# Fetching the embedded rows of five steps by indirect transfers instead of one-hot products

## The reference, cut to what matters

```
h = take(weight.T, x)                                   # (64, 128, 64)
# attention over the heads (h = 8), on the layer-normalised h, no softmax over keys:
q, k, v = (ln(h) @ Wq, ln(h) @ Wk, ln(h) @ Wv)
attn = sigmoid(einsum('bifh,bjfh->bijh', q, k) * 8)
h = h + relu(einsum('bijh,bjfh->bifh', attn, v) @ Wo)
# mixture of 6 experts, 2 per token, on the layer-normalised h:
gates = softmax(top2(softmax(relu(ln(h) @ Wr1 + b) @ Wr2 + b)))
h = h + sum over the 2 chosen experts of gate * expert(ln(h))   # 3 layers of 64 x 64
```

## Time and profile before

| | us |
|---|---|
| median of three runs | 260.37 (257.58 to 261.57) |
| the profiled execution: its own time | 258.21 |
| its span, first to last instruction | 256.4 |
| end of the first part (last `Htab` instruction ends) | 111.96 |
| DVE's `variance` of iterations 2, 3, 4, 5, 6 starts at | 148.03, 162.18, 176.79, 191.16, 205.01 |

### The profile page before, as it was taken

One profiled execution on the slowest core, in us unless ns is written; L12 is line 12 of the kernel. 1 busy time (PEld: TensorE's weight loads), 2 busy tenths in 40 slices (PEclk: granted clock), 3 DMA queues, 4 the chain that ended last, 5 costly groups with the idle time before them and its releaser, 6 DMA issues.

```text
span 256.4 us, 5843 instructions
## 1 busy us (share of the span) xinstructions
PE 206.5 (81%) x2356; PEld 87.8 (34%) x2356; DVE 161.7 (63%) x331; ACT 104.3 (41%) x188; POOL 80.9 (32%) x122
## 2 busy tenths in 40 slices
PE   0559775899899899954837688999899979999882
PEld 0336431234335343344616142524234323232220
DVE  4352852335977857963586488887979685754261
ACT  1148321233453452502431715556273644534430
POOL 4000664322642633044536071532505050101010
PEclk9999997599999799985577799999999999999998
DMA  7541799999898896200006775393938577594911
GB/s 152 129 144 24 182 228 243 252 251 247 222 256 199 233 254 173 82 0 3 0 1 149 163 181 123 88 215 98 206 95 183 123 158 148 119 186 114 202 36 41
DMA packets 25770, 37.85 MB, mean 148 GB/s; under 512 B 15376, under 2 KB 16592, under 8 KB 25744
## 3 DMA queue, kind: packets, MB, share of 16 engines
q1 hardware_dynamic: 18864, 19.92, 34.8%
q0 software_dynamic: 5216, 16.98, 25.9%
q10 hardware_dynamic: 1664, 0.58, 1.1%
HBM read 17.79 MB, written 2.83 MB: 80 GB/s over the span
## 4 chain that ended last, share of the span: by engine, by line
PE 46%; DVE 19%; DMA 14%; ACT 6%; POOL 5%; issue 5%; SPq 4%; DVEq 0%; ACTq 0%
PE PS L644 10%; PE PS L668 9%; PE PS L807 6%; DMA xb<-ids_scratch 6%; DMA G<-Gs 5%; PE PS L778 5%; PE PS L794 4%; POOL st L388 4%; ACT H L482 3%; DVE lead L1064 2%; DVE Htab L925 2%; SPq L335 2%; PE PS L680 2%; DVE OH L992 2%; DVE st L1026 2%
## 5 line engine op out<-in xcount | busy, mean ns | idle before, releaser
L228 POOL DMA_DIRECT2D G<-Gs x64 | 33.5, 529 | 59.3 <-ACT Gs L466 54.2
L644 PE MATMUL PS<-A,BD 32*32 32x256 f32 x1024 | 35.6, 415 | 9.5 <-ACT Gs L466 7.2
L1043 DVE SCALAR_TENSOR_TENSOR H2g<-PS,nb_s,WB 128x1024 f32<-128x1024 f32 x24 | 30.7, 1280 | 11.2 <-PE PS L794 11.2
L482 ACT ACTIVATE H<-PS,b_s 128x512 f32<-128x512 f32 x48 | 30.2, 681 | 16.6 <-PE PS L778 16.5
L969 DVE COPY Gs<-PS 128x512 f32<-128x512 f32 x32 | 20.9, 686 | 20.6 <-PE PS L644 13.1
L668 PE MATMUL PS<-G,cnt 128*64 128x512 f32 x128 | 32.2, 637 | 0.0
L794 PE MATMUL PS<-H,W2s 64*64 64x512 f32 x192 | 27.0, 634 | 5.7 <-ACT H L482 5.6
L466 ACT ACTIVATE Gs<-PS 128x512 f32<-128x512 f32 x32 | 17.6, 595 | 33.0 <-PE PS L644 30.2
L778 PE MATMUL PS<-X,W1s 64*128 64x512 f32 x96 | 27.7, 655 | 0.7 <-ACT H L482 0.7
L807 PE MATMUL PS<-H2g,W3s 128*64 128x512 f32 x96 | 25.5, 616 | 0.4 <-DVE H2g L1043 0.4
L644 PEld LDWEIGHTS PS<-A,BD 32*32 32x32 f32 x1024 | 16.3, 108 | 25.4 <-issue 11.2
(11 more groups left out here) (112 smaller groups left out, 306.4 us busy)
## 6 DMA issues: line engine op xcount, KB each, us to landing
G<-Gs POOLq DMA_DIRECT2D x64, 256.0 KB, 6.4
WB<-gate_scratch SPq DMA_DIRECT2D x16, 768.0 KB, 7.7
xb<-ids_scratch SPq DMA_DIRECT2D x8, 256.0 KB, 7.4
h_out<-Y SPq DMA_DIRECT2D x8, 256.0 KB, 7.0
GG<-gate_scratch SPq DMA_DIRECT2D x64, 12.0 KB
vo_scratch<-VOs SPq DMA_DIRECT2D x2, 256.0 KB, 2.1
VOr<-vo_scratch SPq DMA_DIRECT2D x4, 128.0 KB, 3.0
wk_s<-wk SPq DMA_DIRECT2D x2, 128.0 KB, 4.7
```

Of the source, the lines that this page charges most:

```text
L228: eng.dma_start(G2[half % G2_RING][first::8, :, :], Gs[n % GS_RING][:, m, :]).then_inc(sent[n % GS_RING][m], 16)
L482: ins = act.activation(H1[q][:, u * HT:(u + 1) * HT], PS[:, B_L1 + u, :], ACT.Relu, bias=b1_s[:, u, q:q + 1])
L644: ins = pe.matmul(PS[32 * x:32 * x + 32, B_G + i, w * NV:(w + 1) * NV], BD[n % BD_RING][rows, x].rearrange("p c f -> p (c f)")[:, w::2], A ...
L1043: dve.scalar_tensor_tensor(out=H2g[q][:], in0=two_banks(l2_bank(q)), scalar=nb2_s[:, q:q + 1], in1=WB[s % RING][:, q, :], op0=ALU.max, op1 ...
```

## The change

The one-hot product is kept for steps 0, 1 and 2 (`ON_PE = 3`). For steps 3 to 7:

- SP stores the part of `Htab` that belongs to sequences 24 to 63 in device memory (`h_scratch`, two transfers of 1.31 MB), as soon as the table is complete and ahead of all transfers of the loop.
- DVE computes row numbers once (`row_of` = id x 40 + sequence - 24).
- POOL fetches: `fetch(i + 3)` in iterations 0 to 4, each eight indirect transfers of 128 rows of 256 bytes, straight into `H2` in float32. `centre(i)` and POOL's `normalise(i - 1)` wait for all eight to have landed.
- Gone for these five steps: `gather`, `take_h`, `one_hot_ids`, `x_load` and `cut`; `Hmid`, `Hlo` and `rem` are made for 24 of the 64 sequences only.

Besides: `H2` has eight buffers in place of five; `WB` is loaded by six transfers of 256 KB in place of two of 768 KB, with a semaphore per pair of experts; PE issues `router(i)` ahead of `gather(i + 2)`; and in iterations 0 and 1 DVE issues `normalise(i + 1)` behind `two_best(i)`.

```diff
@@ -61,11 +62,13 @@
 RING = 4
-H_RING = 5
-
-
-C_ID, C_IOTA, C_MASK, C_SEL, C_BM, C_TIE, C_CA, C_CB, C_END = (
-    0, 128, 130, 138, 138 + 192, 334, 370, 370 + NC, 370 + 2 * NC)
+ON_PE = 3
+NBP = ON_PE * TB
+NBD = NB - NBP
+
+
+C_ID, C_IOTA, C_MASK, C_SEL, C_BM, C_TIE, C_CA, C_CB, C_ROW, C_END = (
+    0, 128, 130, 138, 138 + 192, 334, 370, 370 + NC, 370 + 2 * NC, 370 + 2 * NC + NBD)
 A_BITS, B_BITS = 0x33, 0xCC
@@ -78,6 +81,7 @@
     gate_dram = nc.dram_tensor("gate_scratch", (RING, E, TOK), F32, kind="Internal").ap()
+    h_dram = nc.dram_tensor("h_scratch", (NV * NBD, D), F32, kind="Internal").ap()
     ids_dram = nc.dram_tensor("ids_scratch", (1, NB * S), BF16, kind="Internal").ap()
@@ -95,7 +99,8 @@
         Htab = sb("Htab", [P, VK, NB, D])
-        Hmid, Hlo = sb("Hmid", [P, VK, NB, D], BF16), sb("Hlo", [P, VK, NB, D], BF16)
+        Hmid, Hlo = sb("Hmid", [P, VK, NBP, D], BF16), sb("Hlo", [P, VK, NBP, D], BF16)
+        row_of = sb("row_of", [P, NBD], U32)
         rb1_s = sb("rb1_s", [P, 1])
@@ -125,7 +130,7 @@
         O1 = [sb(f"O1{i}", [P, 512], F32, att) for i in range(2)]
-        rem = sb("rem", [P, VK, NB, FB], F32, att)
+        rem = sb("rem", [P, VK, NBP, FB], F32, att)
         G2 = [sb(f"G2{i}", [P, FB, NV], F32, att) for i in range(2)]
@@ -149,7 +154,7 @@
         rem_s = [sb(f"rem_s{i}", [P, VK, TB, FB]) for i in range(2)]
-        H2 = [sb(f"H2{i}", [P, TB, D]) for i in range(H_RING)]
+        H2 = [sb(f"H2{i}", [P, TB, D]) for i in range(STEPS)]
         xc = sb("xc", [P, TB, D])
@@ -307,15 +314,17 @@
             x_load(sp, 2)
+            sp.wait_ge(h_tab, NF * 4 * VK)
+            for k in range(VK):
+                sp.dma_start(h_dram[k * P * NBD:(k + 1) * P * NBD].rearrange("(p b) f -> p (b f)", b=NBD),
+                             Htab[:, k, NBP:, :].rearrange("p b f -> p (b f)")).then_inc(h_st, 16)
             for i in range(STEPS + LAG):
                 if i < STEPS:
-                    if i + 3 < STEPS:
-                        sp.wait_ge(oh_b, VK * (i + 2))
-                        x_load(sp, i + 3)
                     sp.wait_ge(gt_sb, i + 1)
                     if i >= RING:
-                        sp.wait_ge(wb_ld[i % RING], 32 * (i // RING))
+                        for q in range(PAIRS):
+                            sp.wait_ge(wb_ld[i % RING][q], 32 * (i // RING))
                         sp.wait_ge(gg_ld[i % RING], 128 * (i // RING))
@@ -323,10 +332,10 @@
                         sp.wait_ge(gp_ready, i - RING + 1)
-                    for e in range(2):
-                        src = gate_dram[i % RING].rearrange("(q e) k -> e q k", e=2)[e:e + 1]
-                        sp.dma_start(WB[i % RING][e * D:(e + 1) * D, :, :],
-                                     src.broadcast_to([D, PAIRS, TOK])).then_inc(wb_ld[i % RING], 16)
+                    for q in range(PAIRS):
+                        for e in range(2):
+                            src = gate_dram[i % RING][2 * q + e:2 * q + e + 1].broadcast_to([D, TOK])
+                            sp.dma_start(WB[i % RING][e * D:(e + 1) * D, q, :], src).then_inc(wb_ld[i % RING][q], 16)
                     if i == 0:
@@ -380,12 +389,28 @@
                 pool.wait_ge(ln_dve, 4 * i + 3)
-                pool.wait_ge(cut_pool, 3 * min(i + 1, STEPS - 1))
+                pool.wait_ge(cut_pool, 3 * min(i + 1, ON_PE - 1))
+                if ON_PE <= i + 1 < STEPS:
+                    pool.wait_ge(h_ld[i + 1], 16 * TB)
                 if i - 2 >= LAG:
                     pool.wait_ge(gp_ready, i - 1 - LAG)
                 pool.tensor_scalar(st[:, 2, :], st[:, 1, :], EPS, None, ALU.add).then_inc(ln_pool, 1)
                 pool.wait_ge(ln_pool, 2 * i + 1)
                 pool.tensor_tensor(st[:, 3, :], st[:, 2, :], mhalf[:], ALU.pow).then_inc(ln_pool, 1)
+
+            def fetch(i):
+
+                if i == ON_PE:
+                    pool.wait_ge(rows_ok, 1)
+                    pool.wait_ge(h_st, 16 * VK)
+                if i - 3 >= LAG:
+                    pool.wait_ge(gp_ready, i - 2 - LAG)
+                else:
+                    pool.wait_ge(ln_pool, 2 * (i - 1))
+                for t in range(TB):
+                    pool.indirect_dma_start(H2[i][:, t, :], None, h_dram,
+                                            bass.IndirectOffsetOnAxis(row_of[:, i * TB - NBP + t:i * TB - NBP + t + 1], 0))\
+                        .then_inc(h_ld[i], 16)
@@ -405,12 +430,8 @@
                         .then_inc(gp_ready, 1)
-                if i + 3 < STEPS:
-                    if s >= 0:
-                        pool.wait_ge(gp_ready, s + 1)
-                    else:
-                        pool.wait_ge(ln_pool, 2 * (i + 2))
-                    cut(i + 3)
+                if ON_PE <= i + 3 < STEPS:
+                    fetch(i + 3)
@@ -536,7 +555,7 @@
                     relu1(s + 1, 0)
-                if i + 2 < STEPS:
+                if i + 2 < ON_PE:
                     take_h(i + 2)
@@ -827,10 +846,10 @@
                     layer2(s, 0)
-                if i + 2 < STEPS:
-                    gather(i + 2)
                 if a:
                     router(i)
+                if i + 2 < ON_PE:
+                    gather(i + 2)
                 if b:
@@ -873,6 +892,8 @@
                    .then_inc(oh_ready, 1)
+            dve.scalar_tensor_tensor(out=row_of[:], in0=xt_i[:, NBP:], scalar=float(NBD), in1=cst[:, C_ROW:C_ROW + NBD],
+                                     op0=ALU.mult, op1=ALU.add).then_inc(rows_ok, 1)
             dve.wait_ge(ld_ids, 16)
@@ -950,7 +971,7 @@
                     dve.wait_ge(lo_ok, VK * (q - 1) + k + 1)
-                dve.tensor_tensor(rem[:, k], Htab[:, k, :, f], upper(Htab[:])[:, k, :, f], ALU.subtract)\
+                dve.tensor_tensor(rem[:, k], Htab[:, k, :NBP, f], upper(Htab[:])[:, k, :NBP, f], ALU.subtract)\
                    .then_inc(rem_ok, 1)
@@ -1015,11 +1036,14 @@
             def centre(i):
-                dve.wait_ge(h_sb, i + 1)
-                dve.tensor_reduce(st[:, 0, :], H2[i % H_RING][:], AX.X, ALU.add).then_inc(ln_dve, 1)
+                if i < ON_PE:
+                    dve.wait_ge(h_sb, i + 1)
+                else:
+                    dve.wait_ge(h_ld[i], 16 * TB)
+                dve.tensor_reduce(st[:, 0, :], H2[i][:], AX.X, ALU.add).then_inc(ln_dve, 1)
                 dve.wait_ge(ln_dve, 4 * i + 1)
                 dve.scalar_tensor_tensor(out=xc[:], in0=over(st[:, 0, :], D), scalar=-1.0 / D,
-                                         in1=H2[i % H_RING][:], op0=ALU.mult, op1=ALU.add).then_inc(ln_dve, 1)
+                                         in1=H2[i][:], op0=ALU.mult, op1=ALU.add).then_inc(ln_dve, 1)
@@ -1036,8 +1060,7 @@
                 dve.wait_ge(l2_ps, PAIRS * s + q + 1)
-                if q == 0:
-                    dve.wait_ge(wb_ld[s % RING], 32 * (s // RING + 1))
+                dve.wait_ge(wb_ld[s % RING][q], 32 * (s // RING + 1))
                 if s >= 1 and q == 0:
@@ -1118,8 +1141,8 @@
                     gate2(s, 0)
-                if ahead:
-                    normalise(i + 1)
+                    if ahead:
+                        normalise(i + 1)
                 if a:
@@ -1128,12 +1151,12 @@
                     gate2(s, 2)
+                else:
+                    normalise(i + 1)
                 if a:
                     gates(i)
                 if i + 2 < STEPS:
                     centre(i + 2)
-                if i + 3 < STEPS:
-                    one_hot_ids(i + 3)
                 if b:
```

More of the change, by code:

```diff
@@ L22 @@
 I32 = mybir.dt.int32
+U32 = mybir.dt.uint32
 ALU = mybir.AluOpType
@@ L194, in build @@
         oh_b, h_ps, h_sb = sem("oh_b"), sem("h_ps"), sem("h_sb")
+        rows_ok, h_st = sem("rows_ok"), sem("h_st")
+        h_ld = {i: sem(f"h_ld{i}") for i in range(ON_PE, STEPS)}
         rem_ok, mid_ok, lo_ok, cut_dve, cut_pool = (sem(n) for n in ("rem_ok", "mid_ok", "lo_ok", "cut_dve", "cut_pool"))
@@ L200, in build @@
         gate_st = [sem(f"gate_st{i}") for i in range(2)]
-        wb_ld = [sem(f"wb_ld{i}") for i in range(RING)]
+        wb_ld = [[sem(f"wb_ld{i}{q}") for q in range(PAIRS)] for i in range(RING)]
         gg_ld = [sem(f"gg_ld{i}") for i in range(RING)]
@@ L487, in take_h @@
                 act.wait_ge(h_ps, i + 1)
-                if i >= H_RING:
-                    act.wait_ge(y_sb, i - H_RING + 1)
-                act.activation(H2[i % H_RING][:].rearrange("p t f -> p (t f)"), PS[:, B_H, :], ACT.Copy)\
+                act.activation(H2[i][:].rearrange("p t f -> p (t f)"), PS[:, B_H, :], ACT.Copy)\
                    .then_inc(h_sb, 1)
@@ L1105, in result @@
                                   PS[:, B_Y, :].rearrange("p (j u o) -> p u j o", u=2, o=D),
-                                  H2[s % H_RING][:].rearrange("p (u j) o -> p u j o", u=2), ALU.add).then_inc(y_sb, 1)
+                                  H2[s][:].rearrange("p (u j) o -> p u j o", u=2), ALU.add).then_inc(y_sb, 1)
             cut()
```

(1 more changed line is left out.)

## The result

The changed kernel took 277.95 us at the median (276.58 to 281.99), the kernel before 260.85 (257.58 to 261.57): a ratio of **1.068, 95% interval 1.054 to 1.083**. It is slower, and outside the predicted range.

What follows compares the result with a forecast made beforehand. The loop was taken as bound by a 13.85 us round trip over four engines, not PE's load. The span 256.4 - 0.4 + 1.0 for the clock = 257.0 us gave 258.8 us, range 250 to 271.

Steps and rivals of the forecast that it cites:

- P(6): P(k) is the start of POOL's `normalise` of step k; for step 6, 191.55 us was forecast against 191.93 before.
- the formula's terms: Start of POOL's `normalise` of step 6 as 140.75 + 40T + 5L, five fetches of eight issues and a landing.
- T: POOL's time to issue one indirect transfer, taken as 1.02 us.
- rival 2: POOL's issues become the bound: T = 1.3 gives 270.0 us, T = 1.67 gives 285; chance 0.25.
- L: Time from issue of a fetch's last transfer to its landing, taken as 2.0 us, with 7.0 as the bound.
- Rivals 2 and 3: The second is rival 2; the third: rows land late beside `WB` loads, 268.8 us at L = 4, 283.8 at 7; chance 0.07.
- Rival 1: Indirect issues as cheap as POOL's plain ones, T from 0.53 to 0.78: 250.9 to 253.5 us; chance 0.28.
- Rival 4: DVE's two-input instructions hold up POOL's issues, 12.2 us over five fetches: 271.0 us; chance 0.04.
- The first part: Ahead of the loop, remainders and low parts for 24 sequences in place of 64: -1.0 us, between 0 and 1.5.
- Storing the table: Store of 2.62 MB ahead of the fetches, 11.1 us at 236 GB/s, hidden with 2.4 us to spare.
- The clock: PE without gathers reaches iteration 2's matmuls from longer idle time, at a lower clock: +1.0 us, between 0 and 6.
- Waits that go: DVE's 2.59 us wait for ids in iteration 1 disappears, but the gain isn't seen behind POOL: 0.

Runs made afterwards that it cites:

- The refilled kernel: Changed kernel with 48 gather matmuls an iteration issued again on PE in iterations 1 to 5, into a tile nobody reads; 275.29 us, ratio 1.066.
- the kernel with nothing queued behind the fetch: Changed kernel with POOL's two `normalise` instructions replaced by one DVE add and multiply, power left out, all 40 indirect transfers kept; 249.89 us, ratio 0.959.
- the seven kernels of the table: Changed kernel as is, refilled, without fetch, with plain transfers, with four of eight transfers, with late `WB`, with late `WB` and refilled; 248.28 to 276.56 us.
- early ids: Kernel before with the ids of each step loaded one iteration earlier; 256.69 us, ratio 0.987.
- ids and order: Kernel before with ids loaded one iteration earlier, `router` ahead of `gather(i + 2)`, and ranking ahead of `normalise` in iterations 0 and 1; 253.44 us, ratio 0.976.
- the kernel without the second dip: Changed kernel with the `WB` loads of steps 0 and 1 held back until the rows of steps 3 and 4 have landed; 265.54 us, ratio 1.024.
- the two kernels with the stand-in: Kernel before and changed kernel, each with one DVE add and multiply in place of POOL's two `normalise` instructions; 254.52 us (0.988) and 249.89 us (0.959).
- the kernel with two steps fetched: Changed kernel with only steps 6 and 7 fetched, four transfers in each of iterations 0 to 3, ids asked for early; 266.14 us, ratio 1.024.

## Why the prediction was wrong

The profiled execution gives a span of 274.5 us; the sum was 257.0. Of the 17.5 between them 14.8 lie ahead of P(6) (207.37 against 191.55 and the clock's 1.0) and 2.7 behind it. P(3) was to come at 149.5 and came at 159.56.

- **The mechanism held, its sizes didn't.** `normalise` of steps 2 to 6 was to be released by a fetch. It was in four of the five; P(4) was released by the variance, which the clock had made late. From the end of `normalise(1)` to P(6) the formula's terms add up 17.9 us short: issues 8.8, landing 7.2, gaps between `normalise` or the bias part and the first issue 1.9.
- **The first step that failed: T, the issue of an indirect transfer.** Predicted 1.02, measured 0.94 and 0.30 of gap, so 1.25, with a first issue of 1.1, once 1.4. The nearest rows gave 0.78 for an issue that was in fact 0.94, which is near, but the earlier trace rows held no row with pauses between issues, and none was allowed for. At T = 1.25 the issues become the bound, rival 2: 8.8 of the 17.9 us are theirs.
- **The second: L, the landing.** It was near its low end in quiet iterations (1.6 to 1.7 us of idle time behind the last issue, where 2.0 was taken) and wrong beside `WB` (5.9 and 5.4): 7.2 of the 17.9 us. The step that failed is the sentence that a fetch's last transfer goes out when those loads are through. That holds in the later iterations; in iteration 0 SP issues them from 131.2 to 134.9, and the last transfer is issued at 134.9; in iteration 1 they go out from 148.6 to 152.2 and the last transfer at 153.2. The earlier trace rows had the price, 7.0 at the median. Rivals 2 and 3 came together, and were priced as if only one could.
- **Rival 1** fell with the first issue.
- **Rival 4** is a real mechanism with a small price. Of the 40 issues the first of a batch take 1.08 to 1.13 us, with one exception of 1.40; that one, at 144.01, starts while DVE is in the middle of `nrm`:

```profile
143.76 0.69 DVE L1056 TENSOR_TENSOR nrm<-xc,st 128x512 f32<-128x512 f32 x1 [9.32 <-POOL st L399]
```

The refilled kernel has the same inside a batch, beside `xc`:

```profile
203.99 0.69 DVE L1060 SCALAR_TENSOR_TENSOR xc<-st,H 128x512 f32<-128x512 f32 x1
204.28 1.22 POOL L411 DMA_INDIRECT H<-h_scratch,row_of  x1 [0.30 <-issue]
```

Over the eight traces with indirect transfers, 238 issues follow another one directly. Of these, 229 take 0.94 to 0.98 us, and nine take 1.01 to 1.32; each of the nine, and none of the others, began while one of DVE's two-input instructions (`nrm`, `xc`, `lead`, `beats`) had been running for a while, and the more of it was left, the longer the issue. Where `xc` had begun only some 0.02 us before the issue, the issue took its 0.94. So the rule of the Trainium skill (SBUF — State Buffer, "SBUF: two separate sides"), by which whichever of the two starts first keeps the ports and the other waits, agrees with the traces. But in the changed kernel it lengthened one issue of 40, by 0.3 us, where rival 4 was priced at 12.2 in all: most of DVE's two-input instructions lie elsewhere or start behind an issue. The earlier trace rows could not have shown it, since DVE's copies beside those issues read PSUM.
- **The first part** was to give 1.0 us. DVE's first remainder starts at 108.47 where `Htab` was done at 111.96 in the earlier trace rows, 3.5 sooner. But in the kernel with nothing queued behind the fetch, whose first part is the same, it starts at 111.07. In the seven kernels of the table with this first part (all but the last row) P(0) lies between 115.4 and 118.9, on average 1.8 us ahead of the kernel before (119.3) and its two versions with early ids and with ids and order (118.8 and 117.8). So about 2 of the 3.1 us may be the edit's; with a spread of 3.5 us from one execution to the next that is an estimate.
- **Storing the table** was hidden, and with more to spare than 2.4 us: both transfers were issued by 109.3 and the slower landed 7.5 us after its issue, some 9 us ahead of the first fetch at 125.92. What POOL did in the 0.87 us before that fetch, where 0.28 is usual, the trace doesn't name.
- **The clock** was to cost 1.0, up to 6, and was argued for iteration 2. There it came, behind 8.9 us in which PE was idle, granted 0.65 over the iteration, and cost the 1.0 us by which P(4) was later than POOL's loop alone. What the term left out is the 2.7 us behind P(6), granted 0.79. The sign that was named, a lower level after 155 us, was there as well (0.50 from 162 to 170), without being the main cause: the kernel without the second dip (`WB` after the rows) is still at 1.024.
- **Waits that go** were rightly put at nothing, as long as POOL is last. That they are worth 1.3% by themselves, and 2.5% with the order, was left out: the part of the change that helps, hidden by the part that hurts. The same is true of the gathers removed in the first iterations. The sentence that a gather removed is worth about nothing holds in the loop, where the iteration from P(6) has a gather and takes 13.84. That the cuts lay in POOL's idle time doesn't hold in full: the first of them ran beside DVE's `ex` on the chain and lengthened the iteration from P(5) by 0.5 us. And P(3) - P(0) without fetches is 7.2 us shorter, of which ids and order give 4.7 (24.9 us in the kernel with both and no fetch), so that some 2.6 is left for gathers, one-hots, copies and cuts. POOL's 2.0 us were rightly put into the round trip, but without them it is no shorter (13.98 us in the two kernels with the stand-in).

Open: the kernel's `normalise` waits for the rows of the step ahead to have landed before it touches its own data. A kernel in which POOL works on while rows are under way was not tried, so the 1.7 us an iteration that L costs in quiet iterations are known only by subtraction. What passes in the 0.30 us between issues isn't shown either.

## What to carry to other kernels

Before work moves to an engine that looks idle (32% here), ask what the loop waits for on that engine, and add up its own loop with the new work in front: 3.85 + 8 x 1.25 + 1.7 = 15.6 us against a round trip of 13.85. In iterations that have this slack the move is free below the threshold, and above it each microsecond counts; iterations without it (here the first two) have to be added up by themselves. And price a transfer's landing where it stands in the iteration, beside what else is issued then: the same fetch landed in 1.6 us alone and 5.9 us beside 1.5 MB of loads.

## What the runs showed of the hardware

- An indirect transfer of 128 rows of 256 bytes takes POOL 0.94 us and a pause of 0.30 to the next; a plain one of the same bytes 0.53, with no pause. The first of a batch takes 1.1.
- An indirect issue that began while a DVE instruction with two inputs in SBUF was running took longer: 1.40 us at 144.01, beside `nrm`, and 1.57 in the kernel with two steps fetched (144.55, beside `xc`). The same is seen between computing instructions: DVE's `lead` took 0.45 us alone (124.11) and 1.17 beside POOL's bias part (194.78), and the bias part 1.26 alone and 1.70 beside it.
- At a granted clock of 0.51 (its level of 1.2 GHz) the same eight expert matmuls took 1.98 us, at 1.00 (2.4 GHz) 1.09. The clock fell after PE had been busy 2.65 of 5.83 us while it waited for POOL (207.37 to 213.20). But it stayed at 1.00 from 197 to 203 after PE had been busy 2.70 of 6.00 us (192 to 198) in the same waits one iteration earlier, so what decides it isn't shown. This fall was gone with the filler matmuls, and without any filler when the fetches landed sooner.
- Two stores of 1.31 MB, 2.62 MB in all, had landed 7.5 us after issue at the latest, at 334 GB/s over that stretch (108.46 to 116.35); estimated from the 236 GB/s of the earlier trace rows they had been given 11.1.
